# Expert weights copied on chip in the last tiles, q and k sums on GpSimd, third-group gathers without landing waits

## The reference

```python
q = q * cos + rotate_half(q) * sin
k = k * cos + rotate_half(k) * sin
...
scores = jnp.einsum('bthd,bshd->btsh', q, k) * scale
probs = jax.nn.softmax(scores, axis=2)
...
# experts: the two best of 8 by the router, weighted by their softmax
out = p1 * expert_e1(x) + p2 * expert_e2(x)     # expert: relu(x @ W1 + b1) @ W2 + b2
```

## Time and profile before

| | us |
|---|---|
| median of 3 runs | 1623.48 |
| lowest and highest | 1614.8 and 1625.54 |
| span of the profiled execution | 1622.0 |
| TensorE busy in it | 1353.9 |
| ScalarE busy | 990.8 |
| GpSimd busy | 545.8 |

### The profile page before, as it was taken

One profiled execution on the slowest core, in us unless ns is written; L12 is line 12 of the kernel. 1 busy time (PEld: TensorE's weight loads), 2 busy tenths in 40 slices (PEclk: granted clock), 3 DMA queues, 4 the chain that ended last, 5 costly groups with the idle time before them and its releaser, 6 DMA issues.

```text
span 1622.0 us, 26719 instructions
## 1 busy us (share of the span) xinstructions
PE 1353.9 (83%) x8354; PEld 866.5 (53%) x8354; DVE 1095.2 (68%) x2943; ACT 990.8 (61%) x2295; POOL 545.8 (34%) x589
## 2 busy tenths in 40 slices
PE   3466897889888888999999979899899998998681
PEld 1234454534445444666666644467566754687571
DVE  5568879788989898676876895967755754140113
ACT  1354765667676556877777766567568565555430
POOL 2123222313122475212112256435322134344335
PEclk7677998989999889999999998799999999999885
DMA  4012135142321424454544524256555556788772
GB/s 126 7 36 72 42 114 167 46 132 64 110 77 30 121 83 116 139 157 124 168 134 141 154 87 137 78 164 193 159 169 171 159 166 207 225 275 276 225 244 76
DMA packets 202037, 217.68 MB, mean 134 GB/s; under 512 B 17419, under 2 KB 167526, under 8 KB 199593
## 3 DMA queue, kind: packets, MB, share of 16 engines
q1 hardware_dynamic: 193704, 199.18, 41.0%
q0 software_dynamic: 8192, 16.79, 3.4%
HBM read 161.18 MB, written 53.94 MB: 133 GB/s over the span
## 4 chain that ended last, share of the span: by engine, by line
PE 43%; DVE 21%; issue 11%; ACT 8%; POOL 7%; DMA 6%; SPq 2%; POOLq 0%; ACTq 0%; another core or an unknown queue 0%; DVEq 0%
DVE cmx L1581 6%; PE bank L1228 5%; PE bank L1045 5%; PE bank L1028 5%; PE bank L1212 5%; PE bank L1196 4%; PE bank L1151 3%; PE bank L1124 2%; POOL kg L775 2%; DMA kg<-y_slots,sslot 2%; PE bank L1164 2%; PE bank L1013 2%; POOL bhs L775 2%; ACT wide L903 2%; PE bank L1140 2%
## 5 line engine op out<-in xcount | busy, mean ns | idle before, releaser
L1581 DVE TENSOR_REDUCE cmx<-bank 128x2 f32<-128x512 f32 x512 | 328.7, 684 | 97.4 <-PE bank L1196 89.3
L903 ACT ACTIVATE wide<-bank 128x512 f32<-128x512 f32 x512 | 280.0, 609 | 69.2 <-PE bank L1212 64.6
L1212 PE MATMUL bank<-wide 75*128 75x512 bf16 x512 | 174.9, 407 | 23.2 <-DVE cmx L1581 14.7
L1196 PE MATMUL bank<-wide 72*128 72x256 bf16 x1024 | 176.2, 283 | 20.6 <-DVE cmx L1581 15.6
L756 POOL DMA_INDIRECT x_slots<-sx,sslot x128 | 128.1, 1001 | 111.3 <-issue 46.9
L1196 PEld LDWEIGHTS bank<-wide 72*128 72x128 bf16 x1024 | 92.0, 101 | 124.7 <-issue 48.2
L1228 PE MATMUL bank<-wide,bva 128*32 128x512 f32 x1024 | 146.5, 646 | 9.9 <-ACT wide L903 5.7
L942 ACT ACTIVATE mH<-bank,mW 128x128 f32<-128x128 f32 x376 | 107.0, 371 | 57.8 <-PE bank L1028 50.9
L1028 PE MATMUL bank<-mT,mW 128*128 128x128 f32 x872 | 123.8, 287 | 17.0 <-DMA mW<-in_wexp 7.9
L1028 PEld LDWEIGHTS bank<-mT,mW 128*128 128x128 f32 x872 | 112.6, 199 | 36.3 <-issue 14.7
L775 POOL DMA_INDIRECT kg<-y_slots,sslot x88 | 85.9, 976 | 117.9 <-DMA kg<-y_slots,sslot 35.6
(11 more groups left out here) (296 smaller groups left out, 2863.4 us busy)
## 6 DMA issues: line engine op xcount, KB each, us to landing
mW<-in_wexp SPq DMA_DIRECT2D x109, 514.0 KB
wide<-q_parts SPq DMA_DIRECT2D x32, 576.0 KB
inner<-in_wexp SPq DMA_DIRECT2D x31, 514.0 KB
wide<-in_wexp SPq DMA_DIRECT2D x16, 514.0 KB
mX<-x_slots SPq DMA_DIRECT2D x27, 256.0 KB
y_slots<-mX SPq DMA_DIRECT2D x27, 256.0 KB
q_parts<-bp SPq DMA_DIRECT2D x32, 192.0 KB
x_slots<-mH SPq DMA_DIRECT2D x2, 3072.0 KB, 10.9
```

Of the source, the lines that this page charges most:

```text
L903: act.activation(cP[:, i % 8, :], bank[seat["G_s", i]][:, :], ACT.Exp, scale=SCALE).then_inc(S["c_p"], 1)
L1196: ins = pe.matmul(ps[:, j * T:(j + 1) * T], cQ[0:SROWS, z, h, tt * P:(tt + 1) * P], cK[0:SROWS, z, h // G, :], start=True, stop=True)
L1212: pe.matmul(ps[:, :], cK[0:KROWS, z, g, sc_ * P:(sc_ + 1) * P], cQ[0:KROWS, z, h0:h0 + 2, :], start=True, stop=True).then_inc(S["c_s2"], 1)
L1581: dve.tensor_reduce(cmx[:, u % 2, tt, 2 * hp:2 * hp + 2], bank[seat["C_s", i]][:, :].rearrange("p (j t) -> p j t", j=2), AX_X, ALU.max, ne ...
```

## The change

- Weights of the last 50 tiles (106 to 155): a new step M_e loads all eight experts' weights once, one after the other, into `experts`, which takes the place of the score buffer `wide`, after the last product with the probabilities. A new step M_c on VectorE copies a tile's expert from there to the tile's buffer. It reads the offset from `seo`, a third result of S_tile. The late tiles use six buffers throughout, not fourteen.
- q and k sums: k's turned part gets a place of its own, `btk`, and one GpSimd addition over 768 columns (B_add) takes the place of VectorE's two.
- Gathers wait for the landing of the step before only in groups 0 and 1.
- Two multiplications in E_wkv2, and two in G_o, become one.
- The orders are written anew. B_add stands ahead of each chunk's first B_sub; the 50 M_c stand among the last steps of VectorE; SyncE's 8 M_e stand between the loads of tiles 104 and 105; TensorE takes its late products two or three of a kind at a time. Elsewhere steps have mostly changed places with near ones.

```diff
+WAITED_GROUPS = 2
-INNER, WIDE = 4, 8
+INNER = 4
+COPIED_TILE = LATE_TILE + 12
...
-        weights += [wide[:, k * WROW:(k + 1) * WROW] for k in range(WIDE)]
+        experts = wide[:, 0:EXPERTS * WROW]
...
+                    if s == "M_e":
+                        if i == 0:
+                            sp.wait_ge(S["c_pv"], CHUNKS * BC * 4)
+                        sp.dma_start(experts[:, i * WROW:(i + 1) * WROW],
+                                     a["wexp"][i * P:(i + 1) * P, :]).then_inc(S["m_e"], 16)
...
+                    if s == "B_add":
+                        pool.wait_ge(S["b_t"], 3 * i + 3)
+                        pool.tensor_tensor(bqk, bqk, bhs[:, 0:2, :].rearrange("p k n -> p (k n)")[:, 0:QK],
+                                           ALU.add).then_inc(S["b_qk"], 1)
...
-                        if GROUP_OF[c] < GROUPS - 1:
+                        if GROUP_OF[c] < WAITED_GROUPS:
                             landed(s, i)
...
-                        if j:
-                            dve.wait_ge(S["b_t"], 3 * c + 2)
-                            dve.tensor_tensor(bqk[:, 0:N], bqk[:, 0:N], bt, ALU.add).then_inc(S["b_qk"], 1)
...
-                        dve.tensor_tensor(keys, keys, turned, ALU.add).then_inc(S["b_qk"], 1)
...
-                        for j in range(2):
-                            v(dve.tensor_tensor(and_[:, j, :, :], aAB[:, j, :, 0:T], aP[:, 0, :, :], ALU.mult))
+                        v(dve.tensor_tensor(and_[:, :, :, :], aAB[:, :, :, 0:T],
+                                            aP[:, 0, :, :].unsqueeze(1).broadcast_to([P, 2, BC, T]), ALU.mult))
...
+                    if s == "M_c":
+                        t = COPIED_TILE + i
+                        g = place(t)[0]
+                        j = t - FIRST_TILE[g]
+                        k = w_slot(t)[0]
+                        if i == 0:
+                            dve.wait_ge(S["m_e"], 16 * EXPERTS)
+                        dve.wait_ge(S["s_tile"], 3 * (g + 1))
+                        dve.wait_ge(S["m_y"], w_before(t) + 1)
+                        at = dve.value_load(seo[0:1, g, j:j + 1], min_val=0, max_val=(EXPERTS - 1) * WROW)
+                        dve.tensor_copy(weights[k], experts[:, bass.ds(at, WROW)]).then_inc(S[f"m_w{k}"], 16)
```

More of the change, by code:

```diff
@@ L284, in program @@
         bt = bhs[:, 0, :]
+        btk = bhs[:, 1, :]
         QK = N + T
@@ L330, in program @@
         sef = sb("sef", [P, SLOT_TILES])
-        sei = sb("sei", [P, GROUPS, SLOT_TILES], I32)
+        sei, seo = (sb(n, [P, GROUPS, SLOT_TILES], I32) for n in ("sei", "seo"))
         sx = sb("sx", [P, 2, NT, D])
@@ L1940 @@
-        B_ln0s R_m1 E_wkv2 E_rec R_m2 G_o C_s A_c R_e C_s*8 G_o C_s*3 E_att C_s C_mp B_x2 B_ln1s E_x1 C_s*3
-        A_ln1s K_sum K_out E_ln2s R_info B_q*2 B_k G_o E_mix2 C_s*4 G_o B_v K_sum C_s K_out C_s G_y R_ln C_s*3
-        E_mix C_s*4 C_mp R_c E_out E_scan E_y B_ln0s C_s*6 E_wkv E_wkv1 K_sum K_out R_lg G_o R_m1 E_wkv2 E_rec
-        C_s E_att C_s*3 E_x1 C_s E_ln2s C_s*5 C_mp K_sum K_out C_s*5 G_o E_mix2 B_x2 B_ln1s R_m2 R_e G_o C_s
-        K_sum K_out C_s*7 B_q G_o C_s R_info C_s*2 E_out C_mp G_y R_ln B_q C_s*2 B_k C_s R_c B_v B_ln0s C_s*13
@@ L1945 @@
[L1945 to L1949 removed]
+        E_rec A_c E_att E_x1 E_ln2s A_ln1s B_x2 B_ln1s E_mix2 B_q*2 E_mix B_k E_out E_scan E_y B_v B_ln0s E_wkv
@@ new lines @@
+        C_mp A_ln1s C_s*5 E_mix2 C_s*2 B_q*2 B_k G_o C_s*2 B_v C_s*4 G_o C_s*3 C_mp E_mix G_y R_ln C_s*3 E_out
+        C_s*3 R_c E_scan E_y C_s B_ln0s R_lg R_m1 R_m2 R_e A_ln0s G_o R_info C_s*9 E_wkv C_mp E_wkv1 E_wkv2
+        C_s*3 E_rec C_s*2 E_att G_o B_x2 B_ln1s E_x1 A_c E_ln2s A_ln1s G_o C_s B_q C_s*4 B_q G_o C_s*3 E_mix2
+        C_s G_y R_ln C_s*2 B_k C_mp E_mix R_c C_s*2 B_v C_s E_out R_lg R_m1 E_scan R_m2 R_e B_ln0s E_y G_o
+        A_ln0s R_info C_s*6 E_wkv C_s*5 E_wkv1 C_s*2 C_mp E_wkv2 G_o C_s*2 E_rec E_att B_x2 B_ln1s E_x1 E_ln2s
@@ new lines @@
+        E_att A_c E_x1 E_ln2s B_q G_o A_ln1s B_q C_s*2 B_k C_s*3 G_o C_s*6 C_mp E_mix2 G_y R_ln B_v C_s*7 R_c
+        E_out E_mix R_lg B_ln0s R_m1 R_m2 R_e G_o C_s*2 E_scan E_y C_s*5 E_wkv C_s*2 C_mp E_wkv1 E_wkv2 R_info
+        G_o A_ln0s E_rec C_s*2 E_att C_s B_x2 B_ln1s A_c E_x1 E_ln2s A_ln1s G_o B_q*2 C_s B_k E_mix2 C_s*2 B_v
+        C_s*6 G_o C_s*2 G_y C_s*2 R_ln C_mp E_mix R_c C_s*4 E_out C_s B_ln0s E_scan E_y A_ln0s G_o R_lg R_m1
+        R_m2 R_e E_wkv E_wkv1 E_wkv2 C_s*3 E_rec C_s*3 E_att C_s*2 G_o C_s*3 C_mp B_x2 B_ln1s A_c C_s*2 E_x1
@@ new lines @@
+        E_ln2s C_s*3 B_q C_s A_ln1s R_info B_q C_s B_k E_mix2 C_s G_o C_s*6 G_o C_s*2 C_mp E_mix G_y C_s R_ln
+        C_s*2 B_v C_s*2 E_out C_s*2 R_c B_ln0s R_lg R_m1 R_m2 A_ln0s R_e G_o E_scan E_y C_s*6 A_c C_s E_wkv
+        C_s*2 C_mp E_wkv1 R_info G_o E_wkv2 C_s*6 E_rec C_s E_att B_x2 B_ln1s E_x1 E_ln2s A_ln1s C_s*7 B_q C_s*2
+        G_o C_mp E_mix2 G_o G_y C_s R_ln C_s*2 E_mix R_c C_s*3 E_out B_q R_lg R_m1 R_m2 R_e A_ln0s E_scan E_y
+        G_o C_s*3 B_k R_info C_s*2 B_v C_s B_ln0s E_wkv G_o C_s*4 C_mp E_wkv1 E_wkv2 E_rec E_att A_c E_x1 E_ln2s
@@ new lines @@
+        B_ln1s E_x1 C_s*2 A_ln1s K_sum K_out E_ln2s R_info B_q*2 B_k G_o E_mix2 C_s*4 B_v G_o C_s*3 K_sum K_out
+        G_y R_ln C_s E_mix C_s*5 C_mp E_out E_scan B_ln0s R_c E_y C_s*6 E_wkv E_wkv1 K_sum K_out R_lg G_o E_wkv2
+        C_s E_rec E_att C_s*4 E_x1 E_ln2s C_s*2 R_m1 C_s*3 C_mp K_sum C_s K_out C_s*4 G_o E_mix2 B_x2 B_ln1s
+        R_m2 R_e G_o C_s K_sum C_s*3 K_out C_s*4 B_q G_o C_s*2 R_info C_s C_mp E_out G_y R_ln B_q C_s B_k C_s*2
+        R_c B_ln0s B_v C_s*13 C_mp R_lg R_m1 G_o R_m2 R_e G_o R_info C_s*3 G_o B_x2 C_s*2 B_ln1s C_s*5 G_o C_s*6
@@ new lines @@
+        C_mp G_y B_q R_ln C_s B_q C_s*4 R_c C_s*2 B_k C_s*6 B_v C_s*3 C_mp R_lg R_m1 R_m2 R_e R_info S_cnt
+        S_base S_slot G_o S_tile G_o C_s*16 C_mp G_o*2 G_y R_ln C_s*9 R_c C_s*5 G_o C_s*2 C_mp R_lg R_m1 R_m2
+        R_e G_o*2 R_info K_sum K_out G_o M_c*2 G_y R_ln M_c*2 K_sum K_out R_c M_c*2 R_lg R_m1 M_c*2 R_m2 R_e
+        R_info S_cnt S_base S_slot S_tile M_c*5 K_sum M_c*4 K_out M_c*12 K_sum K_out M_c*9 K_sum M_c K_out M_c*4
+        K_sum K_out M_c*4 K_sum K_out M_c*3 K_sum*2 K_out*2 K_sum K_out K_sum K_out
```

394 lines of the change are left out of this document (182 added, 212 removed).

## The result

The changed kernel took **1651.97 us** (median of 4 runs, 1645.25 to 1659.33), the kernel before beside it 1624.51 us: a ratio of **1.0201**, 95% interval 1.0167 to 1.0234. It is slower by 27 us where 32 us less were forecast, and lies 38 us above the upper end of the range. The profiled execution has a span of 1650.6 us.

The account below looks back on a forecast made before the run. TensorE was taken to pace the body, GpSimd's indirect DMA chain and TensorE's weight waits the end. From 1622.0 us, −24 (end) and −7 (body) gave a 1591 us span, forecast 1592 us, range 1577 to 1614.

Parts of the forecast that it names:

- the reordered steps: Body, all engines' new orders: mostly neighbours changing places, value 0, bound ±8 us.
- The addition: Body, q and k sums on GpSimd: first bf16 part 1 us later, cost nothing as readers run ahead; otherwise 16 × 1 us.
- VectorE's relief: Body: 24.5 us net off VectorE, 31% of it counting, gives 8 us.
- The end: After the score work: copied weights and dropped landing waits move both GpSimd's and TensorE's lines, −24 us.
- the two cancel: Last group: S_sc about 9 us later, against 1.8 us off each of five landing waits, 9 us.
- parity: Start of the late tiles: first weight copy at about 1423, level with tile 106's product now at 1423.75.
- both signs of being wrong: End: third group's gathers starting no earlier than 1525, or TensorE ending after 1580, would refute the forecast.
- (2): End: last scatters late, landing waits stay, −15 in place of −24 us, 1601 us; chance 0.22.
- (3): End: copies and K_sum starve each other in one queue, TensorE's end does not move, 1613 to 1616 us; chance 0.09.
- (4): Body: VectorE savings and reordering give more than counted, 1575 to 1585 us; chance 0.09.
- (1): End: VectorE copies block GpSimd's gather issues, 42 us, total 1630, chance 0.08; at half price 1609, chance 0.09.
- The rival on the slower side: End: the rival that copies block GpSimd's gathers, total 1630 us; chance 0.08.

Follow-up runs that it names:

- end-alone kernel: Kernel before with M_e, M_c, the changed slots and waits, and the changed kernel's orders from the last attention chunk on; body as before: 1595.93 us.
- random ScalarE order: 132 neighbouring steps of ScalarE's body order swapped at random, against the kernel with only the end changed (1595.93 us): 1681.41 us.

## Why the prediction was wrong

**The step that failed** is in the body: "the reordered steps are mostly neighbours changing places; their bound is ±8, their value 0". Only about half of the places are two neighbours, and some blocks have up to 28 steps. They cost 55 us. The bound had no row behind it. It took the size of a displacement for the size of its effect, while an in-order queue that stands before one late operand holds up all that follows, on every engine that waits for it. The random swaps, all of neighbours, show the scale for this kernel: +57 and +85 us for some 120 to 130 of them. So neighbours alone are enough to break the bound.

**The addition.** "[I]ts readers are the loads of the next score work, which run ahead, so I cost it at nothing", with 16 × 1 us without the cover. The operation is 1812 ns (1715 forecast from the subtraction). In the old orders the cover is absent: the first bf16 part comes 1.57 us later, 16 times, and the kernel loses 24 to 30 us, beyond that bound. The reader named was the wrong one: B_split itself stands in ScalarE's queue, with B_w1 and the exponentials behind it. Only in the new orders is it as good as free.

**VectorE's relief.** "31% of a saved microsecond counts" gave −8. The joins take 12 us of VectorE's operations away (22.0 to 19.6 and 28.1 to 18.7 us) and gave some −4, which is not clear of the noise; the relief by the additions is not to be seen under either order. In the body VectorE's busy time fell by 12 us (979.8 to 967.4), where 25 were named as the sign; GpSimd's rose by 28, as forecast.

**The end was right**, in size and in mechanism. Forecast −24; measured 1619.4 − 1595.9 = −23.4. The end-alone kernel's body was 9.3 us shorter in the profiled execution (1359.7 against 1369.0), so 9.3 is added here to its times, an estimate of where they would stand behind the old body. First copy forecast at 1423, measured 1417.66 + 9.3 = 1427. First scatter forecast 9 us late, measured 9.3 late; that it stands at 1448.70, nearly where it stood, comes from the shorter body. Behind it the six landing waits that stay up to the third group shrank by 11 us together, where 9 were taken: the two cancel, as argued. Third group's first gather forecast at 1523.8, measured 1515.65 + 9.3 = 1525; fourth group forecast at 1564 by GpSimd's chain alone and 1570 with TensorE's, measured 1563.05 + 9.3 = 1572, behind TensorE's last store (a wait of 4.15 us), so TensorE's line was the longer one, as forecast. The last 23 tiles were forecast at 57.5 us and took 58.3, at full clock. What was not foreseen is the loss ahead of them: parity was forecast for tile 106, and its product comes 16 us later (1430.16 + 9.3 against 1423.75), which the faster tiles behind it make good. A copy with its register load was taken at 1.6 us; it is 1.4 alone (0.71 from the load's start to the copy's, then 0.70) and 0.81 where copies follow each other. In the changed kernel itself both signs of being wrong came (third group's first gather at 1575.40, TensorE's end at 1620), by the later body and not by the end.

**The rivals.** (2) and (3) did not come: the landing waits shrank, TensorE's end moved. Nor did (4): the body gave nothing. (1) is settled by the same trace. In the end-alone kernel, from the first copy on, the 34 gather and scatter issues that overlap a copy take 1.16 us on average and 1.48 at most, the 55 others 0.97: 6.7 us in all, at most 7 forecast, where blocking for the whole of a copy would be 35. The Trainium skill, "SBUF — State Buffer", in its box on the "DVE blocks DMA" trap, has GpSimd's descriptor writing wait until such a copy ends. The trace shows an issue stretched by 0.2 to 0.5 us beside some copies and not at all beside others (0.95 us with a whole copy inside it), so the direction agrees in part, and the cost stays at a fifth of the copies' time. The rival on the slower side had the wrong place: nothing in the list let the body's order lose time. Two slips change nothing: 50 loads are 26.3 MB in the unit in which 8 are 4.2, and by its own times rival (2) is −17, 1599 us.

Faster, same and slower had 0.77, 0.15 and 0.08. All of it rested on the end, where a trace of before has rows to reason from. The body is 80% of the span, its orders were changed on five engines, and no row priced that.

## What to carry to other kernels

When a change rewrites the order of in-order queues, treat the order as a part of its own with a price that the old trace does not give, wide and mostly on the slow side if the old order runs well; find its scale by swapping random neighbours. Bring a local change in with the old order kept, and only then re-plan: here that separates a gain of 28 us (1591.5) from a loss of 27. Ask of every operation moved to another engine what stands behind its first reader in that reader's queue, not only whether the last reader has time.

## What was not expected of the hardware

- A VectorE copy of 128x1028 f32 from SBUF to SBUF has a median of 697 ns, the time of a two-operand addition of 128x512 (692): about 0.68 ns a column, against 0.82 worked out from the scaling of the earlier trace rows. The register load ahead of it, for which 0 to 0.9 us had been allowed, takes 0.3 us and two register steps on VectorE's queue, 0.7 us from its start to the copy's. But the queue does it while the copy before it still runs: copies in a row start 0.81 us apart. VectorE's queue on the line of the load, after (ns min/median/max):

```profile
L1731 DVEq TENSOR_LOAD <-seo x50: 298/304/706, 1476.2 to 1606.2; - x50
L1731 DVEq FUSED_REGOPS  x50: 190/190/216, 1476.8 to 1606.5; - x50
```

- A program with no more instructions and a mean clock in the body that rounds to the same 0.93 can be 55 us slower by order alone. TensorE's busy time holds 18 us of it, all at the lower clock level (159.1 us busy there instead of 141.5); with the random ScalarE order it is busy 211.7 us at that level. So "busy" contains part of the loss, and a mean clock of two digits does not show it.
